# A macaron block on one core: eleven weight chunks ahead of the second expert pass, the last outputs written in another order

## What is computed

```
x = x + 0.5 * ffn(layernorm(x))
x = x + attn(layernorm(x))
x = x + 0.5 * ffn(layernorm(x))
```

## Time and profile before

| | us |
|---|---|
| median of 3 runs | 2319.05 |
| profiled execution, time | 2317.24 |
| profiled execution, span | 2315.5 |
| TensorE (PE) busy | 1981.2 (86%) |
| ACT / DVE / POOL busy | 815.3 / 741.2 / 651.6 |
| HBM read / written | 648.65 MB / 106.43 MB |

### The profile page before, as it was taken

One profiled execution on the slowest core, in us unless ns is written; L12 is line 12 of the kernel. 1 busy time (PEld: TensorE's weight loads), 2 busy tenths in 40 slices (PEclk: granted clock), 3 DMA queues, 4 the chain that ended last, 5 costly groups with the idle time before them and its releaser, 6 DMA issues.

```text
span 2315.5 us, 44186 instructions
## 1 busy us (share of the span) xinstructions
PE 1981.2 (86%) x18664; PEld 1170.8 (51%) x18664; DVE 741.2 (32%) x1248; ACT 815.3 (35%) x1525; POOL 651.6 (28%) x783
## 2 busy tenths in 40 slices
PE   5789999999999999899999999999776556665666
PEld 4546666666666666676666666766421111111111
DVE  6731111111111111567777777677320000000011
ACT  6831111211211211577777777777400000000000
POOL 7610000000000000477777777777311000000002
PEclk9899999999999999999999999999887777878788
DMA  9999999999999999275554444444599999999997
GB/s 368 347 398 414 418 425 422 422 424 420 428 420 422 424 419 390 85 251 179 157 158 150 150 158 156 149 141 151 226 397 425 381 427 427 428 429 427 429 427 305
DMA packets 113556, 762.76 MB, mean 329 GB/s; under 512 B 21704, under 2 KB 21832, under 8 KB 75984
## 3 DMA queue, kind: packets, MB, share of 16 engines
q1 hardware_dynamic: 101264, 701.35, 76.1%
q10 hardware_dynamic: 9216, 50.34, 5.2%
q0 software_dynamic: 2880, 8.25, 0.9%
HBM read 648.65 MB, written 106.43 MB: 326 GB/s over the span
## 4 chain that ended last, share of the span: by engine, by line
PE 56%; DMA 24%; POOL 8%; ACT 6%; issue 4%; SPq 1%; DVE 1%; POOLq 0%; ACTq 0%; DVEq 0%
PE ps L307 52%; DMA big<-in_L_ffn_w 22%; PE ps L311 3%; POOL big L1450 2%; POOL s L1453 2%; DMA last_scratch<-idx 1%; SPq L18 1%; ACT big L590 1%; POOL big L1424 1%; POOL s L1435 1%; ACT big L1276 1%; ACT big L575 1%; POOL big L1455 1%; POOL big L1447 1%; PE ps L770 1%
## 5 line engine op out<-in xcount | busy, mean ns | idle before, releaser
L307 PE MATMUL ps<-big 128*32 128x512 f32 (+4 forms) x13792 | 982.9, 417 | 236.1 <-DMA big<-in_L_ffn_w 195.1
L307 PEld LDWEIGHTS ps<-big 128*32 128x32 f32 (+2 forms) x13792 | 384.5, 127 | 728.1 <-issue 380.3
L315 DVE TENSOR_TENSOR big<-ps,big 128x128 f32<-128x128 f32 (+3 forms) x375 | 343.8, 932 | 694.1 <-PE ps L770 527.2
L307 PE MATMUL ps<-wth,xth 128*128 128x512 f32 x768 | 311.8, 406 | 1.5 <-DVE xtl L315 1.5
L307 PE MATMUL ps<-wtl,xth 128*128 128x512 f32 x768 | 299.6, 390 | 0.0
L307 PE MATMUL ps<-wth,xtl 128*128 128x512 f32 x768 | 299.3, 390 | 0.0
L815 ACT COPY big<-ps 128x512 f32<-128x512 f32 x64 | 37.5, 586 | 656.5 <-PE ps L307 656.5
L1442 POOL TENSOR_SCALAR big<-big 128x1 f32<-128x1 f32 x64 | 12.3, 193 | 846.7 <-ACT ps L1254 844.2
L956 ACT ACTIVATE big<-ps,big 128x512 f32<-128x512 f32 x128 | 88.2, 689 | 371.7 <-PE ps L307 361.9
L965 DVE TENSOR_SCALAR big<-ps,big 128x512 f32<-128x512 f32 x64 | 48.1, 751 | 533.7 <-PE ps L307 533.7
L307 PE MATMUL ps<-wo,s 128*128 128x512 f32 x768 | 210.2, 409 | 3.4 <-ACT big L1324 1.9
(11 more groups left out here) (126 smaller groups left out, 1765.2 us busy)
## 6 DMA issues: line engine op xcount, KB each, us to landing
big<-in_L_ffn_w SPq DMA_DIRECT2D x256, 2048.0 KB, 18.2
p_scratch<-big ACTq DMA_DIRECT2D x64, 768.0 KB, 11.0
big<-p_scratch SPq DMA_DIRECT2D x64, 768.0 KB, 6.0
big<-in_L_attn_x SPq DMA_DIRECT2D x68, 256.0 KB, 3.0
xt_scratch<-big SPq DMA_DIRECT2D x16, 1024.0 KB, 8.4
big<-xt_scratch SPq DMA_DIRECT2D x16, 1024.0 KB, 15.3
x_weight_scratch<-big SPq DMA_DIRECT2D x64, 256.0 KB, 3.3
out_x<-big SPq DMA_DIRECT2D x64, 256.0 KB, 3.5
```

The lines of the kernel that those rows point to most:

```text
L307: return nc.tensor.matmul(o, l, r, start=start, stop=stop, skip_group_check=True)
L315: return nc.vector.tensor_tensor(o, p, q, op)
```

## The change

- **Ring.** A slot becomes a pair of *pieces* of 8 KB per partition (`PIECES`), which need not be neighbours, so three more places exist once before pass 1: places 9, 10 and 11. Place 10 is the area of `MS` and the routing weights `M[0]`, place 11 that of `WOH` and of `KH`, `KL`, `ATH`, `ATL`, place 9 that of the normalised rows. Buffers of attention move: `MS` to the second half of the old `XG` area, `WOL` to address 0, X1 and PB of a pair of tiles into one slot. Chunks 0 to 10 of pass 1 go to the places `FIRST`; from chunk 11 on there are eight slots, in a new order. A chunk whose two pieces lie apart (chunk 6, in place 11) is two transfers; the others stay one.
- **Points of issue.** Chunks 3 and 4 are issued at the start of n = 62, chunk 5 at its end, 6 to 8 behind the loop, then the bias of w1 (into `BO`, no more in wait of the last logits), 9 behind `s_wt`, 10 behind `s_mtok`. `experts_sp` keeps eleven ahead. At the head of attention the loads of `MS` go behind those of X1 and PB, and wait for `s_xsl`, 64.
- **Later steps.** `rank_*`, `pick_*` move from experts 0 to 2 to experts 2 to 4 and wait until chunk 4 is used (its place holds PICK and RANK); the gathers wait for chunk 10; `last_rows_sp` moves from expert 4 to expert 8.
- **End.** `EARLY` is 12: groups 0 to 11 are written as ready. The last chunk comes as two transfers with two semaphores; the matmuls of its first half, and groups 12 to 15, wait for the first alone. The last scatter signals after each half.
- **Mask.** `tensor_scalar(W, W, LOWEST, is_equal)`: one operand, and it no more reads the logits, so in `topk_exp` the exp waits for the replacing and the negated maximum only.

```diff
-        ring = [at(SLOT * i, SLOT) for i in range(8)] + [at(os_at, SLOT)]
+        PIECES = [(SLOT * i, SLOT * i + 2048) for i in range(8)] + [
+            (os_at, os_at + 2048), (xs_at, xs_at + 2048), (xg_at + 2048, m_at), (xg_at, wo_at)]
+
+        def piece(g, k):
+            return at(PIECES[slot_of(g)][k], 2048)
+
...
-        WOH, WOL = (halves(f"wo{i}", xg_at + 2048 * i, 2048).rearrange("p (k n) -> p k n", k=4) for i in range(2))
+        WOH, WOL = (halves(f"wo{i}", p, 2048).rearrange("p (k n) -> p k n", k=4) for i, p in enumerate((xg_at, 0)))
...
-        s = Area(0)
-        MS = [s.take(1024) for _ in range(2)]
-        X1 = [s.take(512) for _ in range(4)]
-        PB = [s.take(1536).rearrange("p (u n) -> p u n", u=3) for _ in range(2)]
-        X2, AT = s.take(512), s.take(512)
-        PB += [s.take(1536).rearrange("p (u n) -> p u n", u=3) for _ in range(2)]
-        QT, KT = s.take(512), s.take(512)
+        s = Area(SLOT // 2)
+        X2, AT, QT, KT = (s.take(512) for _ in range(4))
+        PB, X1 = [], []
+        for _ in range(2):
+            PB += [s.take(1536).rearrange("p (u n) -> p u n", u=3) for _ in range(2)]
+            X1 += [s.take(512) for _ in range(2)]
         ST = s.take(2048).rearrange("p (r n) -> p r n", r=4)
         XT3A = [s.take(512).rearrange("p (k t) -> p k t", k=4) for _ in range(2)]
         L = [at(xs_at, 1024), s.take(1024)]
+        MS = [at(xg_at + 2048 + 1024 * i, 1024) for i in range(2)]
...
-        BS = at(oc_at + 1536, 512)
+        BS = [at(oc_at + 1536, 512), BO]
...
-        EARLY = 8
+        EARLY = 12
...
+            n = g - 4 * E
+            return FIRST[n] if n < len(FIRST) else (4, 5, 6, 1, 7, 2, 0, 3)[(n - len(FIRST)) % 8]
+
+        FIRST = (4, 5, 6, 8, 10, 1, 11, 2, 0, 3, 9)
+        landed, counts = {}, [0] * 8 + [16, 16, 16 * 3, 16 * 2]
+        before, last = {}, {}
         for g in range(8 * E):
-            before[g] = max((h for h in range(g) if slot_of(h) == slot_of(g)), default=None)
-            turns[slot_of(g)] += 1
-            turn[g] = turns[slot_of(g)]
+            q = slot_of(g)
+            before[g] = max((last[p] for p in PIECES[q] if p in last), default=None)
+            last.update((p, g) for p in PIECES[q])
+            counts[q] += 32 if q == 11 else 16
+            landed[g] = counts[q]
...
-            tt(W, L[1][R_, :], W, ALU.not_equal).then_inc(s_top, 1)
+            nc.vector.tensor_scalar(W, W, LOWEST, None, ALU.is_equal).then_inc(s_top, 1)
...
-            act.wait_ge(s_top, 4 * (NR + e - 8) + 4)
+            act.wait_ge(s_top, 4 * (NR + e - 8) + 3)
...
+            dve.wait_ge(s_top, 4 * (NR + b) + 4)
...
-            tt(W, L[0][R_, :], W, ALU.not_equal).then_inc(s_top, 1)
+            nc.vector.tensor_scalar(W, W, LOWEST, None, ALU.is_equal).then_inc(s_top, 1)
...
+            a, b = PIECES[slot]
+            if g == 8 * E - 1:
+                sp.dma_start(piece(g, 0), src[:, 0, :]).then_inc(d_ring[slot], 16)
+                sp.dma_start(piece(g, 1), src[:, 1, :]).then_inc(d_gw, 16)
+            elif b == a + 2048:
+                sp.dma_start(at(a, SLOT).rearrange("p (k n) -> p k n", k=2), src).then_inc(d_ring[slot], 16)
+            else:
+                for k in range(2):
+                    sp.dma_start(piece(g, k), src[:, k, :]).then_inc(d_ring[slot], 16)
...
-                    ahead = 9 if p else 4
+                    ahead = len(FIRST) if p else 4
                     if (g + ahead) // (4 * E) == p:
                         load_chunk(sp, g + ahead)
-                if p == 1 and e == 4:
+                if p == 1 and e == 8:
                     last_rows_sp(sp)
...
+                    v = piece(h, kt % 2)
...
+                    v = piece(h, j % 2).rearrange("p (i n) -> p i n", i=4)
+                    pe.wait_ge(d_ring[slot_of(h)], landed[h])
+                    if h == 8 * E - 1 and j == 3:
+                        pe.wait_ge(d_gw, 16 + 16 * 8 + 16)
...
-                if p == 1 and 1 <= e < 3:
-                    rank_pe(pe, e - 1)
+                if p == 1 and 3 <= e < 5:
+                    rank_pe(pe, e - 3)
...
                 t = mm(ps[:, 6 + half, :], SEL[:, off:off + 128], PT[G % 2], G == 0, G == 7)
-            t.then_inc(s_sel, 1)
+                if half or G == 7:
+                    t.then_inc(s_sel, 1)
...
-            dve.wait_ge(s_sel, 8 * p + 8)
+            dve.wait_ge(s_sel, 9 * p + 8 + h)
...
-            sp.wait_ge(s_used, 4 * E - 3)
-            load_m(0)
+            sp.wait_ge(s_used, 4 * E - 2)
             load_x1(0)
-            load_m(1)
-            for n in range(1, 4):
-                load_x1(n)
-            sp.wait_ge(s_used, 4 * E - 2)
+            load_x1(1)
             load_p(0)
             load_p(1)
             sp.wait_ge(s_used, 4 * E - 1)
+            load_x1(2)
+            load_x1(3)
             load_p(2)
             load_p(3)
+            sp.wait_ge(s_xsl, NT)
+            load_m(0)
+            load_m(1)
             sp.wait_ge(s_o, 2)
...
+                if n == NT - 2:
+                    sp.wait_ge(s_c, NT)
+                    load_chunk(sp, 4 * E + 3)
+                    load_chunk(sp, 4 * E + 4)
...
                 if n == NT - 2:
-                    sp.wait_ge(s_c, NT)
-                    load_chunk(sp, 4 * E + 3)
+                    load_chunk(sp, 4 * E + 5)
...
             sp.wait_ge(s_av, NT)
             sp.wait_ge(s_op, NT)
-            load_chunk(sp, 4 * E + 4)
-            load_chunk(sp, 4 * E + 5)
+            load_chunk(sp, 4 * E + 6)
             sp.wait_ge(s_x2, NT)
-            load_chunk(sp, 4 * E + 6)
+            load_chunk(sp, 4 * E + 7)
             sp.wait_ge(s_x2n, NT)
             sp.wait_ge(d_x2[0], 32 * (NT // 2))
             sp.wait_ge(d_x2[1], 32 * (NT // 2))
-            load_chunk(sp, 4 * E + 7)
+            load_chunk(sp, 4 * E + 8)
+            load_b1(sp, 1)
             sp.wait_ge(s_lg3, NT // 4)
-            load_b1(sp)
             sp.wait_ge(s_wt, NR + 8)
-            load_chunk(sp, 4 * E + 8)
+            load_chunk(sp, 4 * E + 9)
             store_mt(sp, 7)
+            sp.wait_ge(s_mtok, 16)
+            load_chunk(sp, 4 * E + 10)
             sp.wait_ge(s_mg, 16)
             load_b2(sp)
             sp.wait_ge(d_mt, 16 * B)
...
+            pool.wait_ge(s_used, 4 * E + 5)
...
+            dve.wait_ge(s_used, 4 * E + 5)
...
-            pool.wait_ge(s_used, 4 * E + 4)
+            pool.wait_ge(s_used, 4 * E + len(FIRST))
...
-                    pool.wait_ge(d_ring[slot_of(8 * E - 1)], 16 * turn[8 * E - 1])
+                    pool.wait_ge(d_ring[slot_of(8 * E - 1)], landed[8 * E - 1])
```

More of the change, by code:

```diff
@@ L249, in slot_of @@
                 return g % 4
-            return g - 4 * E + 4 if g < 4 * E + 3 else 8 if g == 4 * E + 3 else (7, 2, 0, 1, 3, 4, 5, 6)[(g - 4) % 8]
-        turn, turns = {}, [0] * 8 + [1]
-        before = {}
-        for g in range(8 * E):
-            before[g] = max((h for h in range(g) if slot_of(h) == slot_of(g)), default=None)
-            turns[slot_of(g)] += 1
-            turn[g] = turns[slot_of(g)]
+            n = g - 4 * E
[3 more added lines that the diff above has]
+        before, last = {}, {}
+        for g in range(8 * E):
+            q = slot_of(g)
[3 more added lines that the diff above has]
+            landed[g] = counts[q]
         ROUNDS = [(0, 2), (2, 4), (4, 6), (6, 7), (7, 8)]
@@ L695, in load_biases @@
         def load_biases(sp):
-            load_b1(sp)
+            load_b1(sp, 0)
             load_b2(sp)
@@ L782, in experts_pe @@
                     h = g + 2 + j // 2
-                    v = ring[slot_of(h)].rearrange("p (j i n) -> p j i n", j=2, i=4)
-                    pe.wait_ge(d_ring[slot_of(h)], 16 * turn[h])
+                    v = piece(h, j % 2).rearrange("p (i n) -> p i n", i=4)
+                    pe.wait_ge(d_ring[slot_of(h)], landed[h])
+                    if h == 8 * E - 1 and j == 3:
+                        pe.wait_ge(d_gw, 16 + 16 * 8 + 16)
                     for q in range(4):
                         t = mm(ps[32 * q:32 * q + 32, k, :], HT[e % 4][:, 128 * q + 32 * j:128 * q + 32 * j + 32],
-                               v[:, j % 2, q, :], e % 4 == 0 and j == 0, e % 4 == 3 and j == 3)
+                               v[:, q, :], e % 4 == 0 and j == 0, e % 4 == 3 and j == 3)
                     if j % 2 == 1:
@@ L859, in experts_dve @@
                     ahead_dve(dve, 2 * e)
-                if p == 1 and 1 <= e < 3:
-                    rank_dve(dve, e - 1)
-                if p == 1 and e == 0:
+                if p == 1 and 3 <= e < 5:
+                    rank_dve(dve, e - 3)
+                if p == 1 and e == 2:
                     late_dve(dve)
-                if p == 1 and e < 2:
-                    pick_dve(dve, e)
+                if p == 1 and 2 <= e < 4:
+                    pick_dve(dve, e - 2)
                 if p == 1 and 12 <= e < LAST:
@@ L868, in experts_dve @@
                 if p == 1 and e == LAST:
```

(2 more changed lines are left out.)

19 lines of the change are left out of this document (7 added, 12 removed).

## The result

| | before | after |
|---|---|---|
| median, runs of one comparison | 2318.66 (2317.83 to 2319.84, 4 runs) | 2299.03 (2296.91 to 2302.05, 4 runs) |
| profiled execution, time | 2317.24 | 2299.73 |
| profiled execution, span | 2315.5 | 2298.0 |
| DVE / ACT / POOL busy | 741.2 / 815.3 / 651.6 | 734.2 / 815.3 / 647.2 |

All in us. The ratio is 0.9913, 95% interval 0.9900 to 0.9927: 19.6 us less. The forecast was 2302.5, range 2298.5 to 2309. The head start and the tail came out as forecast; the saving was 3 us larger than the sum.

A forecast was written before the change was run, and what follows sets the result against it. Pass 1 was taken to be bound by its weight stream, with POOL bounding the end behind it. Terms -9.8 - 2.5 + 0 + 0 + 0 + 2.5 - 6.7 = -16.5 us took 2319.05 to 2302.5 us, range 2298.5 to 2309.

The forecast's parts named there:

- head start: Ahead of pass 1: two more weight chunks sent while the DMA engines are nearly idle, -9.8 us.
- tail: From the landing of the last chunk to the span's end: 11.5 us instead of 18.2, -6.7 us.
- Step 1: Ahead of pass 1: two more chunks issued in idle DMA time, so the stream has less to move, -9.8 us.
- slower rival: End of attention: stores of X2 queued behind the early chunks land late and hold attention, 2354 us; chance 0.05.
- Step 2: Stream gap at 1684 to 1688, SP waiting for routing weights: chunk 10 covers it, -2.5 us, bounds 0 and 3.5.
- Step 3: Top-k batches: the exp no longer waits for the mask, nothing on the path waits for it; 0, bounds 0 and -1.2.
- Step 4: Pass 1: ranks, gathers and row numbers later, the hole at 1795 only moves behind expert 8; 0, bounds -2 and +3.
- Step 5: `MS` loaded later, `WOL` elsewhere, new slot order: seven chunks stay issued while one is used; 0 us.
- lost head start: Pass 1: a new hole in the stream eats the two chunks and the gap, 12.3 us; 2314.8 us, chance 0.12.
- Step 6: Pass 1: groups 8 to 11 written inside the full stream move the last landing back, +2.5 us, bounds +1.5 and +5.
- Step 7: Behind the last chunk's landing: halved chunk and earlier group writes, 11.5 us instead of 18.2, -6.7; bounds 10.8 and 15.5.
- rival of the held end: End: POOL's stop or group 12's writes delaying the last half's signal make it 15.5 us long; 2306.5 us, chance 0.15.

## Why the prediction was right or wrong

**Step 1, two chunks ahead, -9.8: right.** Undoing it costs 8.6 (8.5 to 8.9 aligned). The stores behind the early chunks landed in time; no DVE row at tiles 62 and 63 waits for one. The slower rival has nothing in the trace.

**Step 2, the gap, -2.5: right.** The hole is gone, chunk 11 left at 1681.70 (forecast about 1683). The share of the DMA engines in the 32 us behind the last store rose from 0.92 to 1.00, which is 2.6 us. Undoing the step costs 1.5 to 1.8 aligned; the medians' 0.7 can't tell that from nothing.

**Step 3, exp and mask, 0 with bounds 0 and -1.2: wrong, and the step that failed.** It measured -3.9 in attention, -4.2 as a kernel of its own. I wrote "nothing on the path waits for it" after looking at who waits for the mask's result. No engine stands idle for it in these tiles. But POOL's power, which starts beside it, is held while it runs, and lies on the chain. The prediction itself put the new form's 0.69 us beside the old 1.22, and the row with 1.59 us instead of 0.55 for the same 128x1 instruction was in the trace of before; seven such tiles at 0.53 are 3.7. A lower bound of 0.53 x 7 + 1.2 would have taken it in. The other half of the step, an exp that starts earlier, held: it starts 10.8 us behind the last store instead of 12.2, and the stream takes no notice.

**Step 4, the trip of the row numbers, 0: within its bounds, but not 0.** The share of the hole's window is 0.53 over 9 us, 4.2 us, where it was 5.8: -1.6. The gathers stop as before, the 8th for 20.25 us and the 16th for 22.50.

**Step 5, slots and `MS`, 0: right.** Outside that hole, windows stand at 426 and 428 GB/s. The lost head start has nothing in the trace.

**Step 6, groups in the stream, +2.5 with bounds 1.5 and 5: under-costed.** It measured 3.4 to 3.8: these writes took more of the full stream than their bytes, as the upper bound allowed.

**Step 7, the tail, 11.5: right,** 11.4 measured. Group 12 was issued at T - 1.4 (forecast T - 0.5), the last at T + 7.7 (T + 7.8). The rival of the held end didn't come: the last half chunk landed at most 0.9 us later than a whole one, and POOL was idle for 2.90 us ahead of the last rows.

**The sum.** Between the last store and T, -9.9 was measured against -9.8, and that closeness is in part luck, by errors that cancel: the two chunks gave 8.7 instead of 9.8, the writes cost about 3.6 instead of 2.5, and the hole of step 4 gave 1.6 that was put at 0. With step 2 by its share, the terms give -8.7 - 2.6 - 1.6 + 3.6 = -9.3, within the noise of T. With step 2 as undone (-1.6) they give -8.3, and some 1.6 us would have no name. With step 3 at -3.9 the forecast would have been 2298.6. The measured 19.6 is 3.1 more than forecast, and step 3 is more than all of that; 0.9 us the other way lies ahead of attention or between the executions.

**The range and the chances.** The lower end leaves out step 4's -2 and would be 2296.7 with it. The upper end adds one 2.5 to the held end, where the kept gap and the dearer writes are 2.5 each, 2311.5. And 0.68 + 0.15 + half of 0.12 is 0.89, not 0.86, with 0.06 instead of 0.09 left for no difference. None of this changes the account.

## What to carry to other kernels

Before a DVE instruction is costed at nothing because no one waits for its result, look at what runs beside it on POOL: compare the same POOL instruction in iterations with and without it. If it is longer beside the DVE instruction, then that instruction's form and place are on POOL's path, and on the kernel's where POOL is on the chain. Taking out one hold may move the next DVE instruction into another one, so read all of them for the whole period and place them together. And a small transfer that must come back before a queue may go on belongs in another engine's queue than the stream.
